# Moving the first chunk's routing by one unit and spreading four stores on the SyncE queue

## Time and profile before

| what | value |
|---|---|
| median of three runs | 535.0 us |
| the profiled execution | 535.76 us, of which 533.8 us are the span of the trace |
| granted TensorE clock | 1.000 over the span |
| VectorE, ScalarE, GpSimd busy | 78%, 75%, 51% |
| chain that ended last | TensorE 81%, VectorE 7%, ScalarE 4%, issue 3%, DMA 2%, GpSimd 1%, SyncE 1% |

### The profile page before, as it was taken

How to read it: one execution, slowest core, us unless ns; L and a number is a source line. 1 busy time by engine, 2 the same in 40 slices (tenths; PEclk the granted TensorE clock), 3 DMA queues, 4 the chain that set the end, 5 groups by cost and what they waited for, 6 DMA issues and landing times.

```text
span 533.8 us, 8658 instructions
## 1 busy us (share of the span) xinstructions
PE 525.8 (99%) x2663; PEld 431.8 (81%) x2663; DVE 413.7 (78%) x939; ACT 402.2 (75%) x805; POOL 274.4 (51%) x243
## 2 busy tenths in 40 slices
PE   8999999999999999999999999999999999999997
PEld 6577787887888888799989999878887788878876
DVE  6898688877976588867777889779778867976574
ACT  7898878778777776876666657778778777877773
POOL 2879767784876774000000000267676775756753
PEclk9999999999999999999999999999999999999999
DMA  7657576557556750000000000155566666766764
GB/s 251 224 192 223 162 199 208 174 197 194 198 175 187 208 197 4 2 1 0 1 2 2 0 1 1 44 193 168 175 201 192 185 189 194 202 172 193 194 210 136
DMA packets 66526, 75.40 MB, mean 141 GB/s; under 512 B 28080, under 2 KB 32304, under 8 KB 66480
## 3 DMA queue, kind: packets, MB, share of 16 engines
q1 hardware_dynamic: 66032, 74.58, 46.3%
q10 hardware_dynamic: 448, 0.26, 0.2%
HBM read 71.14 MB, written 3.67 MB: 140 GB/s over the span
## 4 chain that ended last, share of the span: by engine, by line
PE 81%; DVE 7%; ACT 4%; issue 3%; DMA 2%; POOL 1%; SPq 1%; POOLq 0%; DVEq 0%; ACTq 0%
PE lrow L1260 12%; PE lrow L1262 11%; PE lrow L1261 11%; PE bank L1310 9%; PE bank L1312 9%; PE bank L1311 9%; PE bank L1377 5%; PE bank L1590 3%; PE bank L1592 3%; PE bank L1591 3%; DMA wide<-gates_dram 2%; DVE gated L774 1%; ACT gpart_hi L508 1%; POOL gpart_lo L310 1%; DVE gpart_lo L310 1%
## 5 line engine op out<-in xcount | busy, mean ns | idle before, releaser
L310 POOL TENSOR_TENSOR gpart_lo<-gated,gpart_hi 128x512 fp32r<-128x512 f32 x175 | 225.7, 1300 | 159.6 <-ACT gpart_hi L508 158.4
L497 ACT ACTIVATE lrow<-lrow 128x512 f32<-128x512 f32 (+1 forms) x245 | 143.9, 587 | 61.7 <-PE lrow L1262 60.3
L774 DVE TENSOR_TENSOR gated<-lrow,wide 128x512 f32<-128x512 f32 x170 | 115.9, 682 | 54.6 <-ACT lrow L497 42.3
L508 ACT CAST gpart_hi<-gated 128x512 fp32r<-128x512 f32 x175 | 107.3, 613 | 10.2 <-DVE gated L774 9.6
L1310 PE MATMUL bank<-gpart_lo,wdn_hi 128*128 128x512 f32 x246 | 97.9, 398 | 0.0
L1312 PE MATMUL bank<-gpart_hi,wdn_hi 128*128 128x512 f32 x246 | 97.2, 395 | 0.0
L1311 PE MATMUL bank<-gpart_hi,wdn_lo 128*128 128x512 f32 x246 | 96.8, 393 | 0.0
L774 DVE TENSOR_TENSOR lrow<-lrow,wide 128x512 f32<-128x512 f32 x74 | 51.4, 695 | 19.6 <-ACT lrow L497 15.5
L1178 DVE TENSOR_TENSOR pT_lo<-bank,pT_hi 128x512 fp32r<-128x512 f32 x64 | 43.6, 683 | 21.7 <-ACT pT_hi L706 21.7
L310 DVE TENSOR_TENSOR gpart_lo<-lrow,gpart_hi 128x512 fp32r<-128x512 f32 (+1 forms) x82 | 55.8, 681 | 1.1 <-ACT gpart_hi L508 1.1
L706 ACT CAST pT_hi<-bank 128x512 fp32r<-128x512 f32 x64 | 38.0, 594 | 23.9 <-PE bank L1377 23.8
(11 more groups left out here) (287 smaller groups left out, 963.9 us busy)
## 6 DMA issues: line engine op xcount, KB each, us to landing
wide<-gates_dram SPq DMA_DIRECT2D x488, 128.0 KB, 3.0
raw<-in_w_up SPq DMA_DIRECT2D x8, 256.0 KB, 5.9
raw<-in_w_down SPq DMA_DIRECT2D x8, 256.0 KB, 5.7
y_dram<-y_blocks SPq DMA_DIRECT2D x24, 64.0 KB, 2.7
y_tok<-y_dram SPq DMA_DIRECT2D x6, 256.0 KB, 3.9
x<-in_x SPq DMA_DIRECT2D x3, 256.0 KB, 4.2
gates_dram<-gate_blocks SPq DMA_DIRECT2D x24, 32.0 KB, 2.0
out_dram<-x SPq DMA_DIRECT2D x3, 256.0 KB, 3.1
```

Source lines behind the costliest of these rows:

```text
L310: return eng.tensor_tensor(gpart[1][0:m, U % NGP, :], gated_at(U)[0:m, :], gpart[0][0:m, U % NGP, :].bitcast(F32), ALU.subtract)
L497: nc.scalar.activation(dst[0:m, :], hid[U % NH][0:m, :], ACT.Silu).then_inc(s_silu, 1)
L508: nc.scalar.copy(gpart[0][0:m, U % NGP, :], gated_at(U)[0:m, :]).then_inc(s_ghi, 1)
L774: nc.vector.tensor_tensor(gated_at(U), a, b, ALU.mult).then_inc(s_gated, 1)
```

## The change

There are three edits.

1. A function `shift(n)` is 1 in chunk 0 and 0 in all others. In chunk 0 `normed` for the next chunk comes two units later on VectorE (u = 7 and 8), and all of the routing up to `pro_top`, with `weights` on GpSimd (u = 19), one unit later. `pro_sum` (u = 20), `normed_weights` (u = 21), `gate_blocks` and `joint_lo` (u = 24) stay. In `pro_xT` the new expression gives 10 for chunk 0, which had 9, and 8 elsewhere, as before.
2. At the start of chunk 0, ScalarE's two copies of the gates (`pro_cwT`) come behind the high part of unit 2, not ahead of it.
3. In the second layer the four stores of y are three units apart (u = 14, 17, 20, 23, for 14 to 17), the reload of y is at u = 27, for 20, and `add_y` at u = 29, for 24.

```diff
+        def shift(n):
+            return 0 if n else 1
...  SyncE
-                    if 14 <= u < 18 and n % NCH:
-                        store_y(n - 1, u - 14)
-                    if u == 20 and n % NCH:
+                    apart = 1 if n < NCH else 3
+                    if n % NCH and u >= 14 and (u - 14) % apart == 0 and (u - 14) // apart < P // SQ:
+                        store_y(n - 1, (u - 14) // apart)
+                    if u == (20, 27)[n // NCH] and n % NCH:
                         load_y(n - 1)
...  GpSimd
-                            if u == 18:
+                            if u == 18 + shift(n):
                                 weights(n + 1)
...  ScalarE, the start of chunk 0
                             hi_unit(1, n)
+                            hi_unit(2, n)
                             pro_cwT(n)
-                            hi_unit(2, n)
                             silu_unit(4, n)
...  ScalarE, pro_hi; joint_aff, joint_silu, joint_hi and pro_sil in the same way (12, 13, 14, 16)
-                            if u == 9:
+                            if u == 9 + shift(n):
                                 pro_hi(n + 1)
...  VectorE
-                            if u == 5:
+                            if u == 5 + 2 * shift(n):
                                 normed(0, n + 1, c + 1, xn[f], p_rs, p_xn, (0, 1))
-                            if u == 6:
+                            if u == 6 + 2 * shift(n):
                                 normed(0, n + 1, c + 1, xn[f], p_rs, p_xn, (2, 3))
...  pro_lo (9), pro_aff (13, 14), reciprocal (14, 15) and pro_top (16, 17) get + shift(n)
-                            if u == (19, 24)[f]:
+                            if u == (19, 29)[f]:
                                 add_y(n - 1, c - 1)
...  TensorE; joint_product (11) and joint_turn (13) get + shift(n)
-                            if u == (8 if n else 9):
+                            if u == 8 + 2 * shift(n):
                                 pro_xT(n + 1)
```

More of the change, by code:

```diff
@@ L655, in _ @@
                         if c + 1 < NCH:
-                            if u == 9:
+                            if u == 9 + shift(n):
                                 pro_hi(n + 1)
-                            if u == 12:
+                            if u == 12 + shift(n):
                                 joint_aff(n + 1)
-                            if u == 13:
+                            if u == 13 + shift(n):
                                 joint_silu(n + 1)
-                            if u == 14:
+                            if u == 14 + shift(n):
                                 joint_hi(n + 1)
-                            if u == 16:
+                            if u == 16 + shift(n):
                                 pro_sil(n + 1)
@@ L1091, in _ @@
                                 stats(0, c + 1, p_st, (2, 3))
-                            if u == 5:
+                            if u == 5 + 2 * shift(n):
                                 normed(0, n + 1, c + 1, xn[f], p_rs, p_xn, (0, 1))
-                            if u == 6:
+                            if u == 6 + 2 * shift(n):
                                 normed(0, n + 1, c + 1, xn[f], p_rs, p_xn, (2, 3))
-                            if u == 9:
+                            if u == 9 + shift(n):
                                 pro_lo(n + 1)
-                            if u == 13:
+                            if u == 13 + shift(n):
                                 pro_aff(n + 1, 0)
-                            if u == 14:
+                            if u == 14 + shift(n):
                                 pro_aff(n + 1, 1)
                                 reciprocal(n + 1, 0)
-                            if u == 15:
+                            if u == 15 + shift(n):
                                 reciprocal(n + 1, 1)
@@ L1107, in _ @@
                                 joint_lo(n + 1)
-                            if u == 16:
+                            if u == 16 + shift(n):
                                 pro_top(n + 1, 1)
-                            if u == 17:
+                            if u == 17 + shift(n):
                                 pro_top(n + 1, 2)
@@ L1518, in _ @@
                         if c + 1 < NCH:
-                            if u == (8 if n else 9):
+                            if u == 8 + 2 * shift(n):
                                 pro_xT(n + 1)
-                            if u == 11:
+                            if u == 11 + shift(n):
                                 joint_product(n + 1)
-                            if u == 13:
+                            if u == 13 + shift(n):
                                 joint_turn(n + 1)
```

## The result

The changed kernel takes 536.04 us (median of 20 runs, 535.19 to 537.52), the kernel before, run beside it, 534.77 (20 runs, 533.82 to 536.11). The ratio is 1.002, with a 95% interval of 1.0013 to 1.0028: slower by 1.3 us, clear of the noise of 20 runs, but less than the 0.3% that was counted as a difference.

A forecast was written before the change was run, and what follows sets the result against it. Two nearly level bounds were taken: TensorE's own work and SyncE's solid sequence of issues. First layer +1.1 and second layer -0.6 gave +0.5 us, a median of 535.5 us, with a range of 533.6 to 536.8.

The forecast's parts named there:

- the class given 72%: Whole kernel: no change that a measurement can tell, between 533.4 and 536.6 us, 72%.
- The first layer's mechanism: Chunk 0: `pro_sum` waits for `weights`, TensorE arrives late, and +1.1 us is carried to the second layer.
- The second layer's: Second layer: stalls go, TensorE is some 2.0 us early, but the last load holds the end: -0.6 us.
- Edit 1's new wait: Chunk 0, unit 20: `pro_sum` waits for `weights` behind GpSimd's low part, VectorE idles 1.5 us, `up` 24 +1.46 us.
- The fourth rival: Chunk 0: `pro_sum`'s wait in full, gate 19 at 43.9 or later, `up` 24 2.0 us late; 536.7 us, 14%.
- The q and k product: Near 66 us: TensorE arrives at 67.8, later than the loads allow, and no longer waits there (-0.36 us).
- Edit 2's floor: First layer: SyncE's gate loads go out 0.56 us later, so the product at 66.67 starts at 67.2: at least +0.5 us.
- Of 2.0 us only 0.6 is kept: End of second layer: TensorE is early, but the last load still starts at 521.91, so the last gate gains 0.6 us.
- the other end, +0.5: Last chunk, u = 29: `add_y` meeting GpSimd's low parts was priced 0, at worst +0.5 us.
- gates 30 and 31 have about that in hand: Last chunk: `add_y` may make gate 30 1.0 us late, but the gates have about that much slack; priced 0.
- the rival that priced this part at -2.0: Second layer keeps its whole gain, -2.0 us, as spread stores disturb fewer loads, with the first layer at +0.5; 533.5 us, 12%.
- The first rival: Whole kernel: SyncE is no bound, all TensorE stalls come back, 3.0 to 6.0 us off, 530.3 us; 7%.

The follow-up runs named there:

- half the issues: Kernel before with one gate load per unit, not two (second expert's gates left out): 534.02 us against 534.81; the whole change on that kernel: 534.54 us.
- the last combination: Kernel before plus edit 1 with `weights` ahead of GpSimd's low part of unit 19, and `add_y` at 29 (28 in the last chunk): 534.11 us against 534.81.
- the one of 1450 us: One load per unit carrying both experts' rows, in place of two loads, against the kernel before: 1450.16 us, ratio 2.7128.

## Why the prediction was right, and what was off

The time of 536.04 lies in the range (533.6 to 536.8), on the side forecast (+0.5; measured +1.3), and in the class given 72%. The first layer's mechanism was right, and its term 0.3 us too high. The second layer's was right in part only, and by the medians its term was 0.8 to 1.2 too low. The two errors go opposite ways, and the larger one alone is as much as the 0.8 us between forecast and result: that the total still lay in the range is owed to the range's width of 3.2 us, not to the sum.

- **Edit 1's new wait: right, a quarter too large.** Gate 19 started at 43.04 (43.3 forecast), VectorE idled 1.50 us (1.5), `pro_sum` started at 46.43 (46.7), `up` 24 at 48.35 (48.7): +1.14 in place of +1.46. Of the 0.32 between, 0.26 are gate 19's, an estimate between 42.3 and 43.9. The fourth rival's condition, gate 19 at 43.9, wasn't met. Taking the wait away took 1.1 us off, and with half the issues the product behind it came 0.83 us late.
- **The q and k product: right.** TensorE came so late that it no longer waited for `turned_lo`; the product started at 67.50 (67.8 forecast, 66.67 before). It took up 0.47 of the delay, 0.36 was forecast. +0.8 of delay went on into the second layer, +1.1 was forecast. (Edit 1 alone carries +0.43 there in its trace and costs 1.1 by the times; an execution and a median differ by that much here.)
- **Edit 2's floor: right at its source.** 19.19 for the first load (19.17 forecast), later loads mostly +0.5 to +0.9 but by no means "every later one 0.56": the one at 26.7 us is as early as before, as the first long issue (last section) comes behind it here and came ahead of it before. Gates wait for loads at 59 to 63 us. Alone it cost 0.4. In the whole change it doesn't add, since it and `pro_sum`'s wait meet at the same product: alone, edits 1, 2 and 3 cost 1.1, 0.4 and 0.6, 2.1 in all, and together 1.3. As the text said, a floor is not a term.
- **Edit 3: the step that failed.** "Of 2.0 us only 0.6 is kept", with `add_y`'s collision priced at 0. The stalls went as said, but the 0.9 behind the gate at 508.29 can't be put down to the stores, as it comes and goes among the kernels whose four stores are as before: absent with edit 2 alone and with `add_y` alone at 29, present in the last combination (0.68 us at 508.23); what is sure are the two stalls of 0.43 behind `add_y`. The count of issues held the last load as said: it started at 522.3, 0.4 later than before. The last gate was not released by it, however, but by VectorE: 525.76 and not 525.3. There `add_y` took 1.61 us (1.80 in chunks 5 and 6), above the 0.85 and 1.37 of the earlier trace rows from which the other end, +0.5, was worked out. The pair with half the issues has it in the open: the last gate goes from +0.07 to +0.38. So "gates 30 and 31 have about that in hand" was wrong by 0.3. The larger loss was a load: in the changed kernel TensorE falls back 0.46 us at 517.77, and with edit 3 alone 0.77, behind gate 25's late load, which the sum doesn't have. By the medians the -0.6 is thus +0.2 to +0.6, and the rival that priced this part at -2.0 is out.
- The first rival is out: nothing near 530.3 came up. Its 4.7 us lie between the 3.0 and 6.0 of the stalls, but no working leads to them.
- What would have shown it wrong (`up` 24 before 47.5, a last load issued before 521) did not come. One of its signs for right did not either: the last gate was not released by its load.

Two things stay open. What edit 3 costs in the whole change is not known to better than a microsecond: the traces say -1.0, the pair with half the issues -0.5, and the medians of edit 3 alone +0.2 to +0.6. And the load for gate 25 of the last chunk is explained in part. Its second half is issued at 512.30 (512.37 before), ahead of the reload, and takes 4.0 us in place of 3.03, and 4.2 in the two other kernels with stores three units apart and the reload at 27. In all three a transfer of instructions (last section) starts 1.7 to 1.8 us behind its issue; before, that transfer came 1.4 us later, 1.8 behind the load of unit 26, and it was that one which took 4.0. What moved the transfer from one unit to the other was not tried.

## What to carry to other kernels

If a queue in program order is moved by one step, ask of each consumer that is not moved with it what now stands ahead of its producer on the other engine; here one GpSimd instruction of 1.3 us did it. A queue that issues without a pause turns most of a wait in it into a loss at the end (2.3 of 3.1 us here), so a load that depends on a store needs the landing time (2.8 us here) between them. And taking stalls away upstream wins nothing where the same engine waits later for a second bound: find that one first. Where a VectorE instruction with two SBUF inputs must stand near one of GpSimd's, look which starts first: here 0.04 us behind it cost `add_y` 1.1 us.

## What the hardware showed beside this

- **Contention hurts both sides, and the order decides.** `add_y` takes 0.68 us when it starts ahead of GpSimd's low part (46 times in the fourteen traces). When it starts behind, it ends 1.83 to 1.85 us after GpSimd's instruction began, whatever its own start, that is some 0.55 after that instruction's end (35 times, without exception): 1.80 us when it starts 0.04 behind, 1.61 at 0.23, 1.43 at 0.41, 0.85 at 0.99. So it stands still until GpSimd's instruction is through, and only then does its own work. The other side pays in the same way: a low part that starts 0.22 us behind `add_y` takes 1.62 us in place of 1.29, and a pair of them that `add_y` runs beside takes 3.00 in place of 2.55. The Trainium skill ("SBUF — State Buffer", section "Who interferes with whom") says that a VectorE instruction with two SBUF inputs contends with a GpSimd instruction that reads SBUF; the trace agrees, and adds that the loss is up to 1.1 us on one side and 0.45 on the other. The 2.2 us by which VectorE is busier in the changed kernel are this: 0.95 in each of chunks 5 and 6, 0.24 in the last.
- **Long issues on SyncE, and what goes with them.** The loads of the changed kernel, by its line:

```profile
L396 SPq DMA_DIRECT2D wide<-gates_dram x488: 444/596/1701, 19.2 to 522.3; - x163
```

One issue in some 45 takes 0.9 to 1.9 us in place of 0.60, at about the same places in each trace (DMA 32 to 42, 78 to 82, 116 to 118, and so on, 12 to 15 of them), moved by a few from run to run. In the last chunk it fell on the reload (514.22, 1.12 us) here and on a load of unit 28 (515.57, 1.20) before. The DMA records say what stands beside it. Of the queue of kind "instruction" that the page numbers 8, in the changed kernel in 514 to 515.2 us, then in the kernel before in 515.3 to 516.5:

```profile
q8 instruction: 1, 0.02, 5.0%
...
q8 instruction: 1, 0.02, 5.0%
```

This queue moves 21 blocks of 16 KB in each execution, also in the one of 1450 us, so they follow the program and not the time. In the eleven traces with two loads a unit, 142 of them fell into stretches in which SyncE issued without a pause. In 138 cases an issue that overlaps the block is long, and it ends 0.2 to 0.4 us behind the block's end (0.38 in the median). The loads issued 1.0 to 2.2 us ahead of a block land late too: over 3.7 us in 35% of the cases, against 1% of the loads away from a block. So the long issues come with the fetching of instructions. That they are caused by it is likely from this timing, not tried. In the kernel before they add up to 9.6 us above 0.60 each, in a queue that has nothing to spare. That one load a unit narrows the spread of the times from 1.6 us or more to 0.4 and 0.5 fits: there a block mostly finds SyncE idle, and two or three issues are long.
